# Perceiver block on one core: media scale taken out of the context rows, new row layout, one load a unit

## The reference

```python
x = x + _L0_ffn_ref(_layernorm(x, axis=-1), router_w, router_b, w1, b1, w2, b2)      # 8 experts, 2 a token
x = x + _L1_xattn_ref(ctx_1024, _layernorm(x, axis=-1), mask, Wq, Wkv, Wout, bout, g_media, b_media, g_latent, b_latent)

def _L1_xattn_ref(x, latents, mask, ...):
    xn = layer_norm(x, g_media, b_media)
    ln = layer_norm(latents, g_latent, b_latent)
    q = (ln @ Wq)...  * scale
    kv = jnp.concatenate([xn, ln], axis=1) @ Wkv
    sim = jnp.where(full_mask, max_neg, q . k)
    out = softmax(sim) . v
    return out @ Wout + bout
```

## Time and profile before

| what | value |
|---|---|
| median of 3 runs (1232.39, 1238.15, 1232.39) | 1232.39 us |
| profiled execution, its own time | 1234.57 us |
| its span | 1232.8 us |
| granted clock of TensorE, mean | 0.945 |
| TensorE, VectorE, ScalarE, GpSimd busy | 83, 62, 57, 36% of the span |
| expert loop | 466 to 607 us |
| second cross attention | 641 to 1060 us |

### The profile page before, as it was taken

How to read it: one execution, slowest core, us unless ns; L and a number is a source line. 1 busy time by engine, 2 the same in 40 slices (tenths; PEclk the granted TensorE clock), 3 DMA queues, 4 the chain that set the end, 5 groups by cost and what they waited for, 6 DMA issues and landing times. The chain is left out here.

```text
span 1232.8 us, 38639 instructions
## 1 busy us (share of the span) xinstructions
PE 1026.1 (83%) x14219; PEld 803.3 (65%) x14222; DVE 770.3 (62%) x2816; ACT 703.5 (57%) x1685; POOL 444.0 (36%) x789
## 2 busy tenths in 40 slices
PE   5899999986777356666679999999999999887964
PEld 2677777763666156666657888888888887532443
DVE  2577777764788268999446555555555555455266
ACT  2577777753677325666336555555555555564367
POOL 1121212214653017888504443444334433202042
PEclk8799999988899669999889999999999999998979
DMA  1443233310000724666434554455445544100001
GB/s 50 119 112 76 70 76 74 71 27 1 1 1 2 269 80 113 177 170 162 115 94 109 133 129 121 124 131 132 124 120 129 132 125 116 42 1 0 1 1 35
DMA packets 98303, 109.87 MB, mean 89 GB/s; under 512 B 14561, under 2 KB 86177, under 8 KB 98049
## 3 DMA queue, kind: packets, MB, share of 16 engines
q1 hardware_dynamic: 95680, 103.07, 32.1%
q0 software_dynamic: 2496, 5.12, 1.6%
HBM read 92.79 MB, written 15.34 MB: 88 GB/s over the span
## 5 line engine op out<-in xcount | busy, mean ns | idle before, releaser
L1536 POOL TENSOR_TENSOR d_p<-d_p,d_rtotal 128x289 f32<-128x289 f32 x256 | 170.3, 665 | 246.5 <-DVE d_rtotal L1677 246.5
L1671 DVE CUSTOM_DVE_ANT_0 d_p<-bank,d_low 128x289 f32<-128x289 f32 x256 | 112.4, 439 | 180.6 <-PE bank L1565 180.6
L1635 ACT ACTIVATE d_p<-d_p,d_nmax 128x289 f32<-128x289 f32 x256 | 137.7, 538 | 92.9 <-DVE d_nmax L1671 92.9
L1578 PE MATMUL bank<-d_pT,d_xr 32*128 32x128 f32 x5120 | 160.9, 275 | 0.0
L1565 PE MATMUL bank<-x_keyT,d_q 128*128 128x289 f32 x512 | 154.8, 423 | 2.5 <-DVE d_nmax L1671 1.3
L1578 PEld LDWEIGHTS bank<-d_pT,d_xr 32*128 32x128 f32 x5120 | 148.7, 187 | 8.8 <-issue 1.5
L438 ACT ACTIVATE a_p<-a_p,a_nmax 128x257 f32<-128x257 f32 x256 | 109.4, 499 | 75.8 <-DVE a_nmax L471 75.8
L1685 DVE STREAM_TRANSPOSE d_pT<-d_p 128x320 f32<-128x320 f32 x256 | 128.5, 502 | 1.1 <-POOL d_p L1536 1.1
L471 DVE CUSTOM_DVE_ANT_0 a_p<-bank,a_low 128x257 f32<-128x257 f32 x256 | 93.8, 422 | 42.1 <-PE bank L388 40.1
L1565 PEld LDWEIGHTS bank<-x_keyT,d_q 128*128 128x128 f32 x512 | 81.9, 189 | 33.3 <-DVE d_nmax L1671 17.9
L1643 ACT ACTIVATE d_a<-bank,x_affine 128x512 f32<-128x512 f32 x64 | 44.0, 687 | 85.2 <-PE bank L1578 85.2
(11 more groups left out here) (334 smaller groups left out, 2119.3 us busy)
## 6 DMA issues: line engine op xcount, KB each, us to landing
d_xr<-key_rows SPq DMA_DIRECT2D x256, 160.0 KB, 3.1
d_low<-mask_low SPq DMA_DIRECT2D x64, 144.5 KB, 3.5
a_ctT<-in_ctxT SPq DMA_DIRECT2D x64, 128.5 KB, 2.1
a_low<-mask_low SPq DMA_DIRECT2D x64, 128.5 KB, 3.1
c_ct<-in_ctx SPq DMA_DIRECT2D x64, 128.0 KB
key_rows<-c_ct SPq DMA_DIRECT2D x128, 64.0 KB
c_w<-in_L_ffn_w SPq DMA_DIRECT2D x8, 578.0 KB, 9.7
c_w<-expert_out SPq DMA_DIRECT2D x8, 256.0 KB, 4.4
```

The lines of the kernel that those rows point to most:

```text
L1536: nc.gpsimd.tensor_tensor(p, p, rtotal[:, b % 2, g:g + 1].broadcast_to([128, KEYS]), ALU.mult).then_inc(normed, 1)
L1578: ins = nc.tensor.matmul(O[j], xr[rows, b % 2, k, :], pT[rows, b % 2, :, 32 * k:32 * k + 32], start=(k == 0), stop=(k == BLOCKS - 1))
L1635: nc.scalar.activation(p, p, ACT.Exp, bias=nmax[:, b % 2, g:g + 1], scale=-1.0, accum_out=total[:, b % 2, g:g + 1]).then_inc(exp_made, 1)
L1671: nc.vector.tensor_tensor_reduce(P[:, b % 2, g, 0:KEYS], S[u % 2], low[:, b % 4, :], -1.0, 3.4e38, ALU.add, ALU.min, accum_out=nmax[:, b % ...
```

## The change

The media factor is no longer multiplied into the rows. In the expert loop `widen` is gone; GpSimd instead normalises one of the four tiles of each unit (`normalise` on GpSimd, signalled by `scaled`), and VectorE the other three. Whoever used the rows waits for both. ScalarE's copy to `keyT` applies the factor as its scale. The copy of the token rows (`copy_x`) moves from VectorE to ScalarE, ahead of relu. The host lays out the context in the order (half, r, k), so that turned tiles already have their columns in the order of `keyT` and the copy is contiguous; the store then writes r outermost. A unit is loaded by one transfer of 256 KB.

In the cross attention the stored rows lack the factor, so TensorE sums the latents' block apart, into `OL`; ScalarE copies that with the offset to `latent_part`, and VectorE forms factor x `O` + `latent_part` (`combine`), which now releases `O` and completes `a`.

```diff
 def load_unit(sp, u):
-            for b in range(2):
-                rows = t["ctx"][(2 * u + b) * CTX:(2 * u + b) * CTX + 256, :].rearrange("(k p) d -> p k d", p=128)
-                sp.dma_start(ct[:, u % RING, 2 * b:2 * b + 2, :], rows).then_inc(ct_loaded[u % RING], 16)
+            sp.dma_start(ct[:, u % RING], t["ctx"][512 * u:512 * u + 512, :].rearrange("(m p) d -> p m d", p=128)).then_inc(ct_loaded[u % RING], 16)
...
             def store_unit(u):
-                sp.wait_ge(normed, u + 1)
+                sp.wait_ge(centred, u + 1)
+                sp.wait_ge(scaled, min(u + 1, UNITS))
...
                 for b in range(2):
                     for k in range(2):
-                        rows = cx.rows_dram[2 * u + b:2 * u + b + 1, 16 * k:16 * k + 16, 0:8, :].rearrange("b k r d -> (b k) r d")
+                        rows = cx.rows_dram[2 * u + b, :, 4 * k:4 * k + 4, :].rearrange("k r d -> r k d")
                         sp.dma_start(rows, ct[:, u % RING, 2 * b + k, :]).then_inc(cx.rows_stored[u % RING], 16)
...
-            def widen(u):
-                rows, tiles = rows_of(u)
+            def normalise(u):
                 at = slot_of(u)
-                pool.wait_ge(centred, u + 1)
-                nc.gpsimd.tensor_tensor(ct[0:rows, at, 0:tiles, :], ct[0:rows, at, 0:tiles, :],
-                                        cx.media[0:rows, 0, :].unsqueeze(1).broadcast_to([rows, tiles, 128]), ALU.mult).then_inc(normed, 1)
+                pool.wait_ge(rooted, u + 1)
+                nc.gpsimd.tensor_scalar(ct[:, at, 3, :], ct[:, at, 3, :], moments[:, at, 3, 0:1], rstd[:, at, 3:4],
+                                        ALU.subtract, ALU.mult).then_inc(scaled, 1)
...
             def keep_keys(u):
...
-                    keys = cx.keyT[:, 2 * u:2 * u + 2, 0:256].rearrange("p b (r k) -> p b k r", r=8)
-                    src = TC[u % 2].rearrange("p (b k r) -> p b k r", b=2, r=8)
-                nc.scalar.activation(keys, src, ACT.Identity, bias=cx.affine[:, 1:2]).then_inc(kept, 1)
+                    keys, src = cx.keyT[:, 2 * u:2 * u + 2, 0:256], TC[u % 2].rearrange("p (b c) -> p b c", b=2)
+                nc.scalar.activation(keys, src, ACT.Identity, bias=cx.affine[:, 1:2], scale=cx.affine[:, 0:1]).then_inc(kept, 1)
...
+            copy_x(0)
             for s in range(SLOTS):
+                if s + 1 < SLOTS:
+                    copy_x(s + 1)
                 relu(s)
...
-                for m in range(tiles):
+                for m in range(min(tiles, 3)):
                     ins = v.tensor_scalar(ct[0:rows, at, m, :], ct[0:rows, at, m, :], moments[0:rows, at, m, 0:1], rstd[0:rows, at, m:m + 1],
...
                 def means(i, b, first=False):
...
-                    for k in range(BLOCKS):
+                    for k in (*range(BLOCKS - 2), BLOCKS - 1, BLOCKS - 2):
                         for j in range(4):
                             rows = slice(32 * j, 32 * j + 32)
-                            ins = nc.tensor.matmul(O[j], xr[rows, b % 2, k, :], pT[rows, b % 2, :, 32 * k:32 * k + 32], start=(k == 0), stop=(k == BLOCKS - 1))
+                            latents = k == BLOCKS - 2
+                            ins = nc.tensor.matmul((OL if latents else O)[j], xr[rows, b % 2, k, :], pT[rows, b % 2, :, 32 * k:32 * k + 32],
+                                                   start=(k == 0 or latents), stop=(k == BLOCKS - 1 or latents))
...
+                def means(i, b):
+                    n = i * EIGHT + b
+                    act.wait_ge(o_made, n + 1)
+                    if n >= 1:
+                        act.wait_ge(o_copied, n)
+                    nc.scalar.activation(latent_part[:], core.bank[:, 2:6, 128:256], ACT.Identity, bias=affine[:, 1:2]).then_inc(latents_copied, 1)
...
+                def combine(n):
+                    dve.wait_ge(latents_copied, n + 1)
+                    if n % 4 == 0 and n >= 8:
+                        dve.wait_ge(out_made, n // 4 - 1)
+                    nc.vector.scalar_tensor_tensor(a[:, n // 4 % 2, :, n % 4, :].rearrange("p (j g) q -> p j g q", j=4),
+                                                   core.bank[:, 2:6, 0:128].rearrange("p j (g q) -> p j g q", g=GROUPS), affine[:, 0:1],
+                                                   latent_part[:].rearrange("p j (g q) -> p j g q", g=GROUPS), ALU.mult, ALU.add).then_inc(o_copied, 1)
...
                         if not (first and u < 2):
                             turn(i, u - 2, first)
+                        if g == 1 and i * EIGHT + b >= 2:
+                            combine(i * EIGHT + b - 2)
                         if b % 4 == 1 and g == 1 and not first:
                             project(i, (b - 9) // 4)
...
-           "ctx": a["ctx_1024"].reshape(BATCH * CTX, D), "ctx_last": a["ctx_1024"][:, CTX - 1, :],
+           "ctx": a["ctx_1024"][:, :256].reshape(BATCH, 32, 2, 4, D).transpose(0, 2, 3, 1, 4).reshape(BATCH * 256, D), "ctx_last": a["ctx_1024"][:, CTX - 1, :],
```

More of the change, by code:

```diff
@@ L1054, in experts_0 @@
             sem(f"c_{n}") for n in ("x_turned", "x_kept", "w1_kept", "up_made", "relu_made", "down_made", "y_kept"))
-        measured, summed, logged, rooted, centred, normed, turned, kept = (
-            sem(f"c_{n}") for n in ("measured", "summed", "logged", "rooted", "centred", "normed", "turned", "kept"))
+        measured, summed, logged, rooted, centred, scaled, turned, kept = (
+            sem(f"c_{n}") for n in ("measured", "summed", "logged", "rooted", "centred", "scaled", "turned", "kept"))
         parts_loaded = [sem(f"c_parts_loaded{n}") for n in range(NCH)]
@@ L1142, in _ @@
                 gather(s)
-            pool.wait_ge(affine_loaded, 48)
             pool.wait_ge(rows_made, 1)
@@ L1149, in _ @@
                     scatter(s - 2)
-                if 1 <= s <= UNITS + 1:
-                    widen(s - 1)
+                if 1 <= s <= UNITS:
+                    normalise(s - 1)
         @block.tensor
@@ L1189, in turn @@
                 rows, tiles = rows_of(u)
-                pe.wait_ge(normed, u + 1)
+                pe.wait_ge(centred, u + 1)
+                pe.wait_ge(scaled, min(u + 1, UNITS))
                 if u >= 2:
@@ L1267, in relu, with copy_x @@
                                          bias=w1[:, s % 3, HID + k:HID + k + 1]).then_inc(relu_made, 1)
+            def copy_x(s):
+                act.wait_ge(x_turned, s + 1)
+                if s >= 2:
+                    act.wait_ge(up_made, s - 1)
+                nc.scalar.activation(xsT[:, s % 2, :], XT[s % 2][:, 0:128], ACT.Copy).then_inc(x_kept, 1)
             def root(u):
@@ L1316, in copy_weights @@
                 v.tensor_copy(w1[:, s % 3, :], w[:, bass.ds(at, HID + KCH)]).then_inc(w1_kept, 1)
[L1318 to L1322, removed]
             def copy_y(s, at):
@@ L1332, in measure @@
                 at = slot_of(u)
-                dve.wait_ge(ct_loaded[at], 16 if u == LAST else 32 * (u // RING) + 32)
+                dve.wait_ge(ct_loaded[at], 16 if u == LAST else 16 * (u // RING) + 16)
                 for m in range(tiles):
@@ L1425, in _ @@
             copy_weights(0, at[0])
-            copy_x(0)
             for s in range(SLOTS + 1):
@@ L1431, in _ @@
                     copy_weights(s + 1, at[s + 1])
-                    copy_x(s + 1)
                 if 1 <= s <= UNITS + 1:
@@ L1478, in cross_attention_1 @@
         nmax, total, rtotal = (sb(f"d_{n}", [128, 2, GROUPS]) for n in ("nmax", "total", "rtotal"))
-        a = sb("d_a", [128, 2, HEADS, 4, LAT])
+        a, latent_part = sb("d_a", [128, 2, HEADS, 4, LAT]), sb("d_latent_part", [128, 4, 128])
         S = [core.bank[:, n, 0:KEYS] for n in (0, 1)]
-        O = [core.bank[:, 2 + j, 0:128] for j in range(4)]
+        O, OL = ([core.bank[:, 2 + j, n:n + 128] for j in range(4)] for n in (0, 128))
         Q, OUT = core.bank[:, 6, :], core.bank[:, 7, 0:128]
@@ L1489, in cross_attention_1 @@
         o_made, o_copied, out_made, out_added = (sem(f"d_{n}") for n in ("o_made", "o_copied", "out_made", "out_added"))
+        latents_copied = sem("d_latents_copied")
         with nc.Block() as block:
@@ L1589, in project @@
                     for h in range(4 * r, 4 * r + 4):
-                        ins = nc.tensor.matmul(OUT, wvo[:, h, :], a[:, ago % 2, h].rearrange("p b q -> p (b q)"), start=(h == 0), stop=(h == HEADS - 1))
+                        ins = nc.tensor.matmul(OUT, wvo[:, h, :], a[:, ago % 2, 4 * (h % 4) + h // 4].rearrange("p b q -> p (b q)"), start=(h == 0), stop=(h == HEADS - 1))
                     if r == 3:
@@ L1636, in exponential @@
                                          accum_out=total[:, b % 2, g:g + 1]).then_inc(exp_made, 1)
-                def means(i, b, first=False):
-                    act.wait_ge(o_made, i * EIGHT + (b + 1))
-                    if b % 4 == 0 and not (first and b < 8):
-                        act.wait_ge(out_made, i * 2 + (b // 4 - 1))
```

(9 more changed lines are left out.)

## The result

The changed kernel takes 1252.75 us as the median of four runs (1250.26 to 1256.91), against 1232.99 of the kernel before on the same chip: ratio 1.0154, 95% interval 1.0114 to 1.0194. That is 19.8 us slower; the forecast was 41 us slower.

| part of the span, us | before | after | difference |
|---|---|---|---|
| up to the first gather of the expert loop | 459.95 | 455.70 | -4.3 |
| from there to the read of the parts | 147.3 | 153.6 | +6.3 |
| from there to the first load of `d_low` | 25.8 | 26.0 | +0.2 |
| from there to the last addition of the cross attention | 427.4 | 440.0 | +12.6 |
| rest | 172.3 | 173.8 | +1.5 |

What follows compares the result with a forecast made beforehand. It took TensorE to bound the attention and GpSimd's 3.77 us slot the expert loop. Four-engine stores cost +30 us, attention +11: 1276 profiled, 1273 us as median, range 1240 to 1302.

Steps and rivals of the forecast that it cites:

- the mechanism of the loop: Expert loop: stores with an outer axis of 4 run on four DMA engines, 5.30 us a slot, +30 us.
- the rate of one engine: Expert-loop stores: each DMA engine moves 17 GB/s, 30 ns a row, so a unit's stores take 3.86 us on four.
- the prediction's own sum for the load of unit 31: Expert loop's last load: 27 stores, 26 loads and 27 slots of gathers on four engines, 142 us after the first store.
- the signs of size: Expert loop: slots of 5.3 us, mean DMA share not above 0.45, loop's end near 637 instead of 607 us.
- taken as hidden: End of the expert loop: the five stores still open take 19 us beside 24 us before the parts are read.
- the slot before: Expert loop before the change: GpSimd's multiplication, gather and scatter make a slot of 3.77 us, 33 of them.
- the attention: Cross attention: VectorE's new operation delays the first projection of each four by 0.66 us, 16 times, plus 0.8: +11 us.
- The sum: Whole kernel: profiled 1234.57 us +30 for the loop +11 for the attention makes 1276, median forecast 1273 us.
- That of sixteen engines: Expert loop: stores stay on sixteen engines, slot 3.2 us, 19 us gained, 11 lost in the attention: 1224 us; chance 0.12.
- GpSimd's tile: Expert loop: GpSimd normalises one 128x128 tile in 0.60 us; near 1.2 us would matter only with sixteen engines, making 1240.
- the prediction's own sum for GpSimd's slot: Expert loop: GpSimd's slot loses 1.28 us of multiplication and gains a 0.60 us tile, 3.77 to 3.09 us.

Runs made afterwards that it cites:

- the two-engine run: Changed kernel with each store cut in two of 64 partitions (2x32x128 on the DRAM side), so two DMA engines carry stores: 1337.95 us, ratio 1.0855.
- the kernel that makes it true: Changed kernel with the store's DRAM side back at 16x8x128, natural host order and strided key copy: 1238.75 us, ratio 1.0057 to the kernel before.
- the kernels without the tile: Against the kernel with sixteen-engine stores and later projection, VectorE normalises all four tiles: 1221.47 us; with the token copy back on VectorE too, 1222.82 us.
- the later projection: Projection one batch later, VectorE's addition two groups later; with sixteen-engine stores, against the changed kernel: 1220.83 us, ratio 0.9909 to the kernel before.

## Why the prediction was wrong

**Right: the mechanism of the loop.** The new store runs on four DMA engines (packet counts), they are full (two engines make it far worse, eight are as good as sixteen), SP's issue is not what bounds (a fourth of the stores on another queue changes nothing), and VectorE's measurement waits for loads.

**Wrong: the rate of one engine.** The step that failed is "I use 17, or 30 ns a row". It was taken from a stretch in which all sixteen engines are busy and from the loop's own bandwidth over its share. An engine that is full while others have room moves some 21.8 GB/s, or 23.5 ns for a row of 512 bytes: that is the rate of the two-engine run, which owes nothing to this kernel's slot. With it the prediction's own sum for the load of unit 31 is 27 x 3.01 + 26 x 0.75 + 27 x 0.38 = 111 us after the first store. Measured: 465.23 to 577.96, 112.7 us. The forecast had 142, 29 us too many. So none of the signs of size came: slots of 4.2 us and not 5.3, a DMA share of 0.54 and not 0.45 or less, the read of the parts at 609 us and not near 637.

**Wrong in smaller ways, and partly offsetting.** The prediction set the issue of unit 31's load (613 us, 30 and not 31 us late) against VectorE's measurement of it (582.78). Between the two lie 4.9 us here (577.96 to 582.90), which it left out; with them the error would have been larger. Counted from the first gather unit 31 is measured 4.4 us later than before, and 1.9 more are lost from there to the read of the parts, which the forecast had taken as hidden: +6.3 measured, +30 forecast. And the slot before was taken at 3.77 us, GpSimd's ordinary one. SP's loads were then 3.90 us apart on the mean between 480 and 560 us, since some slots are longer; now it is 4.26.

**Right: the attention.** 16 x 0.66 = 10.6 and 0.8 at the end were forecast, 0.66 a first step and +12.6 us for the stretch were measured: 10.4 of them between the first and the last addition (703.7 to 1075.3, before 699.3 to 1060.5), 2.2 ahead of the first. The combination took 708 ns (median), the forecast 0.66 to 0.74. The ordinary step shown above was not touched. What of the 2.2 us ahead of the first addition is the wait of the first projection and what is scatter isn't traced further.

**The sum.** +30 + 11 was forecast; the profile has +6.3 and +12.6, with -4.3 ahead of the loop that is scatter between executions and +1.5 behind. The forecast of 1273 was 20 us too high: the loop's term by 24, the attention's too low by less than 2, the rest is that scatter and the one between runs.

**The rivals.** That of sixteen engines was wrong in its condition, and its price was twice what the loop gives: it had a slot of 3.2 us and 19 us gained; the kernel that makes it true gains 8.1 us of loop (139.2 against 147.3) and is slower than the one before by 0.57%, not faster at 1224. GpSimd's tile was taken at 0.60 us from a row outside the loop and took 0.8 to 1.1 in it. The prediction said this would matter only with sixteen engines, and there it does: at its mean of 0.97 us in that run (480 to 560 us) the prediction's own sum for GpSimd's slot is 3.77 - 1.28 + 0.97 = 3.46 us and not 3.09, and 3.6 was measured. But it isn't the only limit, as the kernels without the tile show. There SP's ordinary slot of 3.18 us and the long slot of every four make 3.5 together, where the prediction had taken the mean of the busiest engine for the slot.

## What to carry to other kernels

Before a transfer's shape is changed, count over how many engines its outer axis can be dealt, on both sides, and compare the time that the fullest engine needs for its bytes with the slot; a mean share of 0.52 hid four full engines here. Take the rate of a single engine from a place where it alone is full, not from the total over sixteen. An operation added on an engine with much idle time costs mostly what waits behind it in that queue: here the repair was not a faster operation but a consumer moved one step later, which also made the kernel before faster.

## What the runs showed of the hardware

One DMA engine with 512-byte rows, most of them from SBUF to DRAM: 21.8 to 22 GB/s when two of sixteen are full, 21.2 to 21.6 when four are; when the sixteen together were at a share of 0.99, 279 GB/s, 17.4 each. What they share then wasn't tried.

VectorE's copy of 128x516 takes longer when GpSimd works on a tile beside it. Three groups by line: before (with the multiplication of 1.28 us, 480 to 576 us), after (same stretch), and sixteen engines without a tile on GpSimd (480 to 560 us):

```profile
L1316 DVE COPY c_w<-c_w 128x516 f32 x26 | 24.5, 942 | 7.8 <-issue 7.8
```

```profile
L1322 DVE COPY c_w<-c_w 128x516 f32 x24 | 10.9, 452 | 7.8 <-issue 6.4 <-ACT c_hs L1264 1.4
```

```profile
L1313 DVE COPY c_w<-c_w 128x516 f32 x22 | 9.3, 421 | 6.9 <-issue 6.9
```

942 ns against 421. In the kernel before, between 480 and 560 us, the 16 copies that overlap a multiplication took 0.54 to 1.27 us and the 5 others 0.43. A copy that starts 0.3 us into the multiplication ends 0.3 us behind it, as one that waits for it would (the multiplication is that of the earlier trace rows, 526.63 to 527.91):

```profile
526.95 1.25 DVE L1316 COPY c_w<-c_w 128x516 f32 x1
```

What the two engines share wasn't tried. GpSimd's tile in turn takes 0.81 us alone and 1.03 to 1.05 beside such a copy and the normalising behind it (sixteen engines). So work taken off GpSimd gave VectorE half a microsecond a slot in the changed kernel, which no sum over one engine's own rows had. With sixteen engines and the tile on GpSimd the copies still take 729 ns on the mean, 527 with the later projection too (both 480 to 560 us).

SP's issue of a store grows when the engines behind it are full: some 0.6 us each with sixteen (2.46 for four), 0.8 in the changed kernel (3.04 to 3.21 for four).
